# Logits from three-part bfloat16 splits at the head of the next turn

## The reference, cut to what matters

```
x = x + gnn(layernorm(x), adj, ...)          # 128 graphs of 128 nodes, D = 256
x = x + ffn(layernorm(x), ...)               # 16384 rows, 16 experts

def ffn(x):
    logits = xf @ switch_w.T + switch_b      # 16 logits per row, in float32
    probs = softmax(logits); route_probs = max(probs); routes = argmax(probs)
    pos = place of the row among the rows of its expert
    keep = pos < capacity
    out = where(keep, expert_w[routes] @ row + expert_b, xf) * route_probs
```

## Time and profile before

| | |
|---|---|
| time, median of 3 runs | 741.64 us (740.81 to 742.03) |
| profiled execution | 743.05 us |
| span of the profiled execution, first to last instruction | 741.3 us |
| TensorE busy | 707.4 us (95% of the span) |
| VectorE busy | 639.5 us (86%) |
| ScalarE busy | 480.8 us (65%) |
| GpSimd busy | 456.6 us (62%) |
| logits matmuls, L1474 | 512, 65.7 us busy; their weight loads 76.5 us busy |

### The profile page before, as it was taken

The page is one execution under the profiler, slowest core; times in us unless marked ns, Lnnn a source line. Parts: engine busy times, 40 slices in busy tenths (PEclk is TensorE's granted clock), DMA queues, the critical chain, the costliest instruction groups (busy, mean ns, idle before and its releaser), DMA issues.

```text
span 741.3 us, 17931 instructions
## 1 busy us (share of the span) xinstructions
PE 707.4 (95%) x4714; PEld 620.0 (84%) x4714; DVE 639.5 (86%) x3129; ACT 480.8 (65%) x1509; POOL 456.6 (62%) x542
## 2 busy tenths in 40 slices
PE   8999999999999999999999999999999999968784
PEld 7888788788998998888989989889888888857673
DVE  6899999999998999999999989999999998867462
ACT  3567677667666667676676766676767667654451
POOL 6446666546666676666666666766666666565554
PEclk9999999999999999999999999999999999987997
DMA  9976565534443454444354334444443322254430
GB/s 283 206 181 159 158 167 155 145 117 149 130 131 124 155 158 152 151 151 148 127 156 139 120 122 154 155 140 152 143 131 135 109 102 90 86 175 144 117 108 6
DMA packets 95458, 104.33 MB, mean 141 GB/s; under 512 B 10729, under 2 KB 85622, under 8 KB 95360
## 3 DMA queue, kind: packets, MB, share of 16 engines
q1 hardware_dynamic: 77104, 65.97, 30.1%
q0 software_dynamic: 15376, 34.30, 14.7%
q10 hardware_dynamic: 2880, 2.92, 1.6%
HBM read 54.13 MB, written 54.76 MB: 147 GB/s over the span
## 4 chain that ended last, share of the span: by engine, by line
PE 86%; DVE 6%; issue 3%; ACT 1%; DMA 1%; POOL 1%; another core or an unknown queue 0%; SPq 0%; POOLq 0%; DVEq 0%; ACTq 0%
PE ps_z12a L1359 11%; PE ps_z12b L1359 11%; PE ps_lgb L1359 9%; PE ps_z0a L1359 8%; PE ps_z0b L1359 7%; PE ps_lga L1474 6%; PE ps_z0a L1442 4%; PE ps_z0b L1442 4%; PE ps_z12b L1421 4%; PE ps_xt L1461 4%; PE ps_xt L1389 3%; PE ps_lgb L1505 3%; PE ps_z12a L1421 3%; PE ps_t L1435 2%; PE ps_t L1410 2%
## 5 line engine op out<-in xcount | busy, mean ns | idle before, releaser
L587 POOL DMA_INDIRECT out<-lent,tok x143 | 145.6, 1018 | 156.2 <-DVE lent L1273 134.7
L574 POOL DMA_INDIRECT rowbuf<-rows,idx x128 | 130.3, 1018 | 52.4 <-issue 27.4
L652 ACT CAST xth<-ps_xt 128x256 fp32r<-128x256 f32 x128 | 47.9, 374 | 95.7 <-PE ps_xt L1389 94.8
L519 POOL TENSOR_SCALAR x<-xin,nm,r 128x256 f32<-128x256 f32 x128 | 84.5, 662 | 16.5 <-PE ps_xt L1389 10.5
L726 ACT ACTIVATE x<-rin 128x255 f32<-128x255 f32 x143 | 86.8, 608 | 3.1 <-DMA rin<-rowbuf 2.4
L1474 PEld LDWEIGHTS ps_lga<-swc,xft 128*128 128x128 f32 x512 | 76.5, 190 | 10.8
L707 ACT ACTIVATE od<-rows,oc,oa 128x256 f32<-128x256 f32 x128 | 77.0, 602 | 0.1
L1474 PE MATMUL ps_lga<-swc,xft 128*128 128x16 f32 x512 | 65.7, 242 | 0.0
L948 DVE TENSOR_TENSOR em<-e 128x128 f32<-128x128 f32 x128 | 40.1, 314 | 26.1 <-ACT e L674 25.1
L868 DVE TENSOR_TENSOR xtl<-ps_xt,xth 128x256 fp32r<-128x256 f32 x128 | 53.9, 421 | 9.4 <-ACT xft L699 7.6
L673 ACT ACTIVATE e<-ps_t,svs 128x128 f32<-128x128 f32 x128 | 47.1, 368 | 22.7 <-PE ps_t L1435 20.6
(11 more groups left out here) (223 smaller groups left out, 2363.1 us busy)
## 6 DMA issues: line engine op xcount, KB each, us to landing
rin<-rowbuf SPq DMA_DIRECT2D x143, 130.0 KB
out<-od SPq DMA_DIRECT2D x32, 512.0 KB
xin<-in_x SPq DMA_DIRECT2D x31, 512.0 KB, 4.4
ain<-in_adj SPq DMA_DIRECT2D x32, 256.0 KB, 4.6
ewr<-in_ewT SPq DMA_DIRECT2D x16, 256.0 KB, 3.9
ewr<-negs POOLq DMA_DIRECT2D x16, 256.0 KB, 5.1
out<-lent,tok POOLq DMA_INDIRECT x143
rowbuf<-rin ACTq DMA_DIRECT2D x1, 2080.0 KB, 20.1
```

Of the source, the lines that this page charges most:

```text
L519: pool.tensor_scalar(x0[:, g % 2, :], xin[:, g % BODY, :], nm1[:, q, g % G:g % G + 1], r1[:, q, g % G:g % G + 1], ALU.add, ALU.mult).then_ ...
L574: pool.indirect_dma_start(out=rowbuf, out_offset=bass.IndirectOffsetOnAxis(ap=idx[:, i:i + 1], axis=0), in_=rows[:, r, :], in_offset=None, ...
L587: pool.indirect_dma_start(out=out.rearrange("g n d -> (g n) d"), out_offset=bass.IndirectOffsetOnAxis(ap=tok[:, i % RY:i % RY + 1], axis=0 ...
```

## The change

The rows' transposed values are split in three bfloat16 parts that add up to the float32 value. ScalarE's copy now rounds to bfloat16 (`xft`), VectorE subtracts that from PSUM into `xfr` (`middle_part`, float32; its upper 16 bits are used as the second bfloat16 part through a strided view, `upper`), and GpSimd subtracts these from `xfr` into `xf3` (`last_part`). The switch weights are split in the same way once (`switch_parts`, on GpSimd in turn 2), so that one product of a part with the weights has 48 columns. The logits of a graph are then six bfloat16 products (three parts, two halves of D) instead of two float32 ones, and VectorE adds the three groups of 16 columns (`lgs`) before it scales them. TensorE does the logits of graph k-4 at the head of turn k, before `turned_rows`, where before it only waited for ScalarE's copy; `turned_rows` now waits for VectorE's remainder.

```
--- before.py
+++ after.py
@@ -154,7 +154,12 @@
         ve2 = sb("ve2", [P, 2, G])
         nm2 = sb("nm2", [P, 2, G])
         swc = sb("swc", [P, KT, E])
-        xft = sb("xft", [P, D])
+        swp = sb("swp", [P, KT, 3, E], BF16)
+        swr = sb("swr", [P, 2, KT, E])
+        xft = sb("xft", [P, D], BF16)
+        xfr = sb("xfr", [P, D])
+        xf3 = sb("xf3", [P, D], BF16)
+        lgs = sb("lgs", [P, G, E])
         lg = sb("lg", [P, G, E])
         mx = sb("mx", [P, G])
         df = sb("df", [P, G, E])
@@ -268,6 +273,10 @@
         s_lgb = sem("s_lgb")
         s_xft = sem("s_xft")
         s_xfe = sem("s_xfe")
+        s_xfr = sem("s_xfr")
+        s_xf3 = sem("s_xf3")
+        s_swp = sem("s_swp")
+        s_lgs = sem("s_lgs")
         s_log = sem("s_log")
         s_lgr = sem("s_lgr")
         s_ro = sem("s_ro")
@@ -321,6 +330,17 @@
         def bat(it, rel):
 
             return it * NB + rel // G
+
+        def upper(v):
+
+            return v.bitcast(BF16).rearrange("p (d h) -> p d h", h=2)[:, :, 1]
+
+        def log_span(b2, j, m=1):
+
+            o = (b2 * G + j) * 3 * E
+            return ps_log[:, o:o + m * 3 * E]
+
+        SWS = slice(2 * G * 3 * E, 2 * G * 3 * E + E)
 
         def xr(i):
 
@@ -524,6 +544,10 @@
                     pool.wait_ge(s_ewn, 1)
                     for t in range(KT):
                         pool.dma_start(negs[:, t, :], ewn[:]).then_inc(d_neg, 16)
+                if it * BODY + k == 2:
+                    switch_parts()
+                if valid(it, k - LAG_XFT):
+                    last_part(it, k - LAG_XFT)
                 rows_first = it * BODY + k >= B - 1
                 i = woven(it, k - 1)
                 if i is not None and not rows_first:
@@ -549,6 +573,22 @@
                     pool.wait_ge(d_ew[e % EPP], 16 * (e // EPP + 1))
                     pool.dma_start(ewr[:, e % EPP], negs[e:e + 1].to_broadcast([P, KT, D]),
                                    accum_op=ALU.add).then_inc(d_ewd[e % EPP], 16)
+
+            def switch_parts():
+
+                pool.wait_ge(s_swc, 1)
+                pool.tensor_copy(swp[:, :, 0, :], swc[:]).then_inc(s_swp, 1)
+                pool.wait_ge(s_swp, 1)
+                pool.tensor_tensor(swr[:, 0], swc[:], swp[:, :, 0, :], ALU.subtract).then_inc(s_swp, 1)
+                pool.wait_ge(s_swp, 2)
+                pool.tensor_copy(swp[:, :, 1, :], swr[:, 0]).then_inc(s_swp, 1)
+                pool.wait_ge(s_swp, 3)
+                pool.tensor_tensor(swp[:, :, 2, :], swr[:, 0], swp[:, :, 1, :], ALU.subtract).then_inc(s_swp, 1)
+
+            def last_part(it, g):
+
+                pool.wait_ge(s_xfr, it * BODY + g + 1)
+                pool.tensor_tensor(xf3[:], xfr[:], upper(xfr[:]), ALU.subtract).then_inc(s_xf3, 1)
 
             def row_factors(it, g):
                 r = g % BODY
@@ -612,8 +652,10 @@
             pool.wait_ge(s_pc, 10)
             phase_a(pool, slot_fn, -LEAD_X0, 1)
 
+            last_part(IT, BODY - 2)
             for g in range(OUT_LEFT - IT * BODY, G30):
                 row_scatter(IT, g)
+            last_part(IT, BODY - 1)
             tokens(IT, G30)
             pool.wait_ge(s_slot, NG - 1)
             row_scatter(IT, G30)
@@ -867,6 +909,8 @@
                         dve.wait_ge(s_xfe, n(k - LAG_XFT))
                     dve.tensor_tensor(xtl[:, g % 2, :], ps_xt[:, 0:D], xth[:, g % 2, :].bitcast(F32),
                                       ALU.subtract).then_inc(s_x0l, 1)
+                if valid(it, k - LAG_XFT):
+                    middle_part(it, k - LAG_XFT)
                 if counts is not None:
                     backlog(counts)
                 if chooses is not None:
@@ -998,6 +1042,12 @@
                 dve.scalar_tensor_tensor(rows[:, r, 0:D], hb[:, g % 2, :], 0.0, xin[:, r, :], ALU.max,
                                          ALU.add).then_inc(s_x1, 1)
 
+            def middle_part(it, g):
+
+                dve.wait_ge(s_xfe, it * BODY + g + 1)
+                ge(dve, s_xf3, it * BODY + g)
+                dve.tensor_tensor(xfr[:], ps_xt[:, D:2 * D], xft[:], ALU.subtract).then_inc(s_xfr, 1)
+
             def row_stats(it, g):
                 dve.wait_ge(s_x1, it * BODY + g + 1)
                 dve.bn_stats(st2[:, g % 2, :], rows[:, g % BODY, 0:D]).then_inc(s_st2, 1)
@@ -1019,16 +1069,18 @@
 
                 dve.wait_ge(s_sws, 1)
                 dve.scalar_tensor_tensor(
-                    swc[:], ps_log[:, 2 * G * E:2 * G * E + E].rearrange("p (o e) -> p o e", o=1)
+                    swc[:], ps_log[:, SWS].rearrange("p (o e) -> p o e", o=1)
                     .to_broadcast([P, KT, E]), -1.0 / D, sw[:], ALU.mult, ALU.add).then_inc(s_swc, 1)
 
             def scaled_logits(it, g):
                 b = bat(it, g)
                 r = g % BODY
                 dve.wait_ge(s_log, b + 1)
+                dve.tensor_reduce(lgs[:], log_span(g // G % 2, 0, G).rearrange("p (g c e) -> p g e c", c=3, e=E),
+                                  AX_X, ALU.add).then_inc(s_lgs, 1)
                 dve.wait_ge(s_r2, b + 1)
-                dve.tensor_tensor(lg[:], per_expert(ps_log[:, g // G % 2 * G * E:(g // G % 2 + 1) * G * E]),
-                                  over_experts(rows[:, r:r + G, RSTD]), ALU.mult).then_inc(s_lgr, 1)
+                dve.wait_ge(s_lgs, b + 1)
+                dve.tensor_tensor(lg[:], lgs[:], over_experts(rows[:, r:r + G, RSTD]), ALU.mult).then_inc(s_lgr, 1)
 
             def add_bias(it, g):
                 b = bat(it, g)
@@ -1301,6 +1353,7 @@
             advanced(c - 1)
             biased_sum(IT, BODY - 1)
             residual(IT, BODY - 1)
+            middle_part(IT, BODY - 2)
             row_stats(IT, BODY - 1)
             row_moments(IT, BODY - 1)
             finish(WOVEN - 1)
@@ -1310,6 +1363,7 @@
             low(WOVEN)
             starts(c)
             passed(c)
+            middle_part(IT, BODY - 1)
             scaled_logits(IT, G31)
             rises(c)
             add_bias(IT, G31)
@@ -1380,7 +1434,7 @@
                 if valid(it, k):
                     pe.wait_ge(s_x0l, n(k))
                 if valid(it, gx - 1):
-                    pe.wait_ge(s_xfe, n(gx - 1))
+                    logits(it, gx - 1)
                 if valid(it, gx):
                     turned_rows(it, gx)
                 if valid(it, g):
@@ -1434,7 +1488,7 @@
                     pe.wait_ge(s_sv, n(k))
                     pe.transpose(ps_t[:, 0:P], svs[:, c, 0:1].to_broadcast([P, P]), ident[:]).then_inc(s_st, 1)
                     times_w(ps_z12[c][:], w12h, w12l, PARTS[4:], True).then_inc(s_z12, 1)
-                if valid(it, gx):
+                if it * BODY + k == B:
                     logits(it, gx)
                 if valid(it, g):
 
@@ -1445,7 +1499,7 @@
                 if it * BODY + k == 1:
                     pe.wait_ge(d_r, 32)
                     for t in range(KT):
-                        mm = pe.matmul(ps_log[:, 2 * G * E:2 * G * E + E], onesf[:], sw[:, t, :],
+                        mm = pe.matmul(ps_log[:, SWS], onesf[:], sw[:, t, :],
                                        start=(t == 0), stop=(t == KT - 1))
                     mm.then_inc(s_sws, 1)
                 if it * BODY + k == B:
@@ -1455,7 +1509,7 @@
                     expert(i)
 
             def turned_rows(it, g):
-                ge(pe, s_xfe, it * BODY + g)
+                ge(pe, s_xfr, it * BODY + g)
                 pe.wait_ge(s_x1, it * BODY + g + 1)
                 for t in range(KT):
                     mm = pe.transpose(ps_xt[:, D + t * P:D + (t + 1) * P], rows[:, g % BODY, t * P:(t + 1) * P],
@@ -1465,14 +1519,17 @@
             def logits(it, g):
                 j = g % G
                 b2 = g // G % 2
-                pe.wait_ge(s_xfe, it * BODY + g + 1)
+                pe.wait_ge(s_xf3, it * BODY + g + 1)
                 if it * BODY + g == 0:
-                    pe.wait_ge(s_swc, 1)
+                    pe.wait_ge(s_swp, 4)
                 if j == 0:
                     ge(pe, s_lgr, bat(it, g))
-                for t in range(KT):
-                    mm = pe.matmul(ps_log[:, (b2 * G + j) * E:(b2 * G + j + 1) * E], xft[:, t * P:(t + 1) * P],
-                                   swc[:, t, :], start=(t == 0), stop=(t == KT - 1), skip_group_check=True)
+                parts_of = [xft[:], upper(xfr[:]), xf3[:]]
+                for n, part in enumerate(parts_of):
+                    for t in range(KT):
+                        mm = pe.matmul(log_span(b2, j), part[:, t * P:(t + 1) * P],
+                                       swp[:, t].rearrange("p c e -> p (c e)"), start=(n == 0 and t == 0),
+                                       stop=(n == 2 and t == KT - 1), skip_group_check=True)
                 if j == G - 1:
                     mm.then_inc(s_log, 1)
 
@@ -1498,7 +1555,7 @@
                 if i == WOVEN + 1:
                     pe.wait_ge(b_fin, WOVEN)
                 if i == WOVEN + 3:
```

(2 more changed lines are left out.)

74 lines of the change are left out of this document (60 added, 14 removed).

## The result

The changed kernel takes 798.31 us (median of four runs, 797.25 to 798.95), the kernel before 741.72 us beside it (740.81 to 742.03). The ratio is 1.0764, with a 95% interval from 1.0745 to 1.0782. The forecast was 775 us, 752 to 800, slower with 0.92. The sign is right and the time lies in the range, 2 us under its upper end, but the loss is 57 us where 34 were summed up. So the working needs a closer look than its range does.

The account below looks back on a forecast made before the run. VectorE was taken to become the bound: 24 groups of four turns at 0.6 + 0.3 us gave 22 us, seven early groups 11, the end 1. Together 34 us on the median of 741.64 gave 775 us, range 752 to 800.

Parts of the forecast that it names:

- a case in which every third part holds VectorE up over the port: Rival: VectorE loses 1.36 instead of 0.3 us per four turns, 33 us more, 808 us; chance 0.12.
- The subtraction: `middle_part` on VectorE, once a turn ahead of `svs`: 0.42 us long, the next instruction 0.34 us after it.
- 1.1 of 1.71: VectorE's added work per four turns, subtractions and sum, is 1.71 us; its idle times were taken to absorb 1.1.
- The sum: VectorE's addition of three column groups, once in four turns: 0.35 us, and the scaling waits for its end.
- my 0.6: Growth of four turns with expert work from VectorE's additions after idle time: 0.6 us, bounds 0.1 and 1.1.
- GpSimd's third part: One subtraction a turn ahead of GpSimd's scatters: 0.65 us plus 0.1 to hand over; scatters' delay priced at nothing.
- What held up `em` before: VectorE's 1.05 us idle before `em`: part called a delay its lateness does not shorten, so half taken as given back.
- The port: GpSimd slows VectorE's steps with two SBUF operands: 0.3 us per four turns added, bounds 0 and 1.36.
- The end: The last graph's logits come 1.4 us later, of which other tail work may hide some: 1 us taken.
- TensorE's products: Six bfloat16 products cost 0.25 us a turn for 0.35 removed; TensorE's 13 us gain was not counted.
- GpSimd becomes the bound: Rival: TensorE waits for the third part at the head; 38 us above the forecast, 813 us; chance 0.05.
- The signs I named: Expected profile: VectorE over 96% busy, TensorE idle before `svs` and `tm` products, four turns 21.4 us, early 18.9, third part 0.6 to 0.8.

Follow-up runs that it names:

- e7: Changed kernel without GpSimd's third part (four products in place of six) and with the logits at the old place of their own turn: 771.63 us, ratio 1.0369.
- e2: Changed kernel without GpSimd's third part, the logits being four products of two parts in place of six of three: 787.40 us, ratio 1.0585.
- e10_both_parts_unused: e1_middle_alone with GpSimd's third part added at the change's place; neither result is used, logits are the old float32 products, no sum: 790.30 us, ratio 1.0618.
- e1_middle_alone: Kernel before with only VectorE's subtraction (`middle_part`) added once a turn at the change's place, result unused: 759.61 us, ratio 1.0209.
- e4_middle_behind_svs: Changed kernel with VectorE's subtraction (`middle_part`) moved right behind `svs` in place of ahead of it: 840.62 us, ratio 1.1297.
- e9: e7 without VectorE's sum over the three column groups as well; two column groups are left out of the logits: 750.15 us, ratio 1.0074.
- e11_products_alone: Changed kernel without both remainders: six bfloat16 products, all on the upper half of ScalarE's float32 copy, at the logits' old place; sum stays: 747.47 us, ratio 1.0046.
- e6: Changed kernel with GpSimd's third part moved behind the `rowbuf` scatter of its turn, ahead of the next row normalization: 852.37 us, ratio 1.1452.

## Why the prediction was right, and where it was not

One way from before to after: the subtraction +16, four bfloat16 products for the float32 ones -9, the sum +21, the third part with its two products +31, the move to the head -2 (no difference within the intervals). Together +57. The last two can be taken the other way round: then the move costs 16 (e7 to e2) and the third part 13 (e2 to the changed kernel). Together they cost 29 either way, and which of them it is put down to depends on the order.

**That the time is in the range is partly luck.** The upper end of 800 was the forecast plus three quarters of a case in which every third part holds VectorE up over the port, 25 us. That did not happen in the changed kernel. The late signals, which were not in the sum, and the group sum of the logits, which was too small in it, took up that room.

- **The subtraction: sized right.** It fills 4 x 0.34 us of the queue in a group and lengthens it by 0.46, so two thirds are hidden. I had given back the same share, 1.1 of 1.71. I had looked for the cover in front of `em`, though. It lies in front of the expert product.
- **The sum: mis-sized.** Its 0.35 us is right, and so is the wait for its end. But beside the subtraction no idle time is left for it in e7_no_third_old_place, and it shifts `wr` onto a scatter: 0.75 us a group, 21 us, where its share of my 0.6 was 0.12. That the same sum costs 4 us in the changed kernel shows that such prices belong to a schedule and not to an instruction.
- **The step that failed: GpSimd's third part, priced at nothing but 0.3 us a group for the port.** "The new wait for VectorE's remainder holds up the scatters by about a microsecond. The transfers behind them are needed turns later, so I price that at nothing" is right of the transfers. I did not ask what the scatter instruction itself does to others while it runs, and so where it stands against TensorE's signals and VectorE's small steps. It costs 31 us with nobody reading the result (e10_both_parts_unused), and 13 in the changed kernel. The part's own length, 0.65 taken, is 0.624. GpSimd had the room that I counted.
- **What held up `em` before: misread.** I took the 1.89 us from `svs` to the first exponential for a delay of the turn with counts, and half of the 1.05 us behind it as lost. 0.76 us of it lie between the transpose of `svs` and the exponential, and that is a late signal:

```profile
479.89 0.97 POOL L574 DMA_INDIRECT rowbuf<-rows,idx  x1 [0.30 <-issue]
...
480.38 0.27 PE L1435 MATMUL ps_t<-ident,svs 128*128 128x128 f32 x1
```

  The transpose ends at 480.65 by the record and the exponential starts at 481.41, 0.55 us behind the end of the scatter (480.86). Of 96 such transposes between 150 and 650 us 22 had a late signal in the kernel before, none in the changed one. So what the forecast lacked could be seen before the change.
- **The port: right as a mechanism, wrong as a term.** In the changed kernel VectorE's instructions last 1.99 us more in a group than before; the subtraction and the sum are 4 x 0.41 + 0.35 = 1.99. So on balance the 0.3 us that I added is nothing there. In e10_both_parts_unused they last 0.96 us a group longer than in e1_middle_alone (0.63 at `tm`, 0.33 at `df`), but the way from `xtl` to `head` is only 0.24 longer and `xth>xtl` 0.20 shorter. I had also read L1113's 409 ns as the price of L519. In the trace each of the 14 long ones of the 15 ends with GpSimd's scatter of `out`, as here at 485.88 and 485.90:

```profile
485.47 0.41 DVE L1113 TENSOR_SCALAR oa<-pr 128x4 f32<-128x4 f32 x1
```

```profile
484.89 1.01 POOL L587 DMA_INDIRECT out<-lent,tok  x1 [3.43 <-DVE lent L1273]
```

  `idx` at 0.50 us in e4_middle_behind_svs and `wr` at 0.56 in e7_no_third_old_place end with the GpSimd instruction beside them as well. By the Trainium skill's SBUF — State Buffer (section "SBUF: two separate sides") a VectorE operation with two SBUF inputs and a GpSimd operation that reads SBUF exclude each other for the whole instruction. `idx` agrees with that. Beside the scatter the trace agrees for a part only: `df`, with two SBUF operands too, starts 0.13 us into the scatter that holds `wr` up and keeps its 0.21 us.
- **The end: 1 us taken, 5 measured.** All runs with the third part have it (129.6 us from turn 124 on, 130.1 in e10_both_parts_unused), those without it do not (124.6 in e1_middle_alone and 124.7 in e2_no_third_part).
- **TensorE's products: 0.16 us, not 0.25.** The six start within 504.61 - 504.45 = 0.16 us, up to the transposes behind them:

```profile
504.45 0.22 PE L1530 MATMUL ps_lga<-swp,xft 128*128 128x48 bf16 x2
...
504.61 0.42 PE L1515 MATMUL ps_xt<-ident,rows 128*128 128x128 f32 x2
```

  That TensorE's gain does not count at all was wrong: 9 us of it do (e1 to e9), or 18 if the sum costs 21 us in e11_products_alone.
- **The rivals.** 808 for "held up by every third part" was nearer to the time than my forecast, and the part is where it put the loss. But of the 0.89 us a group that the part adds by itself, 0.84 lie at `head>xth`, where the late signals are, and not where VectorE is held up. "GpSimd becomes the bound" did not happen: it waits 52 of 320 us for VectorE's remainder.
- **The signs I named.** Idle time of TensorE ahead of `svs` (24.3 us in 320), the third part at 0.6 to 0.8, the early groups at 18.9 (19.25): right. VectorE over 96% busy and four turns of 21.4: wrong, 94% and 21.99 in the middle. The view has no wait of TensorE for `tm`; its second wait is for the expert rows' remainder. A queue that is not full and still sets the time is what a loop of hand-overs looks like.

Left open: why TensorE's signals come late beside the scatter. That they do is read from the traces, and that it makes the 0.84 us rests on where the time lies, on the sums of the lateness, and on the runs without a late transpose (e1, e2, e6, e7). In those 3 to 24 of the 84 to 96 head transposes were due near the end of a scatter and none came late, so the place alone does not make a signal late. No run took the lateness away by itself, so this cause is argued from the traces and not shown by an edit. Moving the subtraction behind `low` was not tried.

## What to carry to other kernels

When several engines are over 85% busy and hand work round in a loop, walk the loop before pricing: which hand-over has slack, and how much. Give it to the first addition only. Where hand-overs in a row are delayed, the price of one addition depends on which others are there, so take it in the kernel that you mean to run. An operation put ahead of a wait in another engine's queue also moves everything behind it in time, so ask what those instructions do to the others while they run, DMA instructions above all, and not only when their data is needed. And price a part by adding it unused: one such run found 31 us where the forecast had 0.3 us for each of 31 groups, 9 us.

## What the runs showed of the hardware

- TensorE's completion signals due from 0.65 us before to 0.55 us behind the end of GpSimd's `rowbuf` scatter can reach their waiter up to 0.9 us late, half of them in the changed kernel (111 of 230). Outside that place none of 609 was over 0.1 us late, though the scatters of `out`, as long, lie there. The record lacks the signals of 111 more matmuls, 98 of them due beside a scatter of `out`; for 54 of them ScalarE stood idle and started 0.04 us behind the matmul, so those were on time.
- A VectorE step with two SBUF operands that starts while a GpSimd scatter or subtraction runs can end with it (0.56 for 0.26 us, 0.50 for 0.13 us). It depends on where in the scatter it starts: in e7_no_third_old_place 22 of 26 `wr`, most of them 0.42 us into it, ended with the `rowbuf` scatter, and of 24 `df`, most of them 0.13 us into it, none lasted longer than 0.22 us.
- GpSimd subtracts 128x256 with two SBUF operands, the second through a bfloat16 view, in 0.62 us in the mean of the changed kernel (0.60 to 0.66); the estimate of 0.55 by the Trainium skill's page (GPSIMD Engine Reference, section 3.1) was without dispatch.
- Six bfloat16 products with 48 columns, two with a strided view as weights, start 0.025 to 0.04 us apart.
